# A four-layer modulated convolution on one core: another opening, with filler matmuls on TensorE

## The reference

```
x = out = input                               # (128, 64, 1024)
for i, typ in enumerate(('same', 'upsample', 'same', 'downsample')):
    s = style @ mod_w[i].T + mod_b[i]         # (128, 64)
    weight = SCALE * w[i] * s[:, None, :, None]
    demod  = rsqrt(sum(weight * weight, axis=(2, 3)) + 1e-8)
    weight = weight * demod[:, :, None, None]
    same:       out = conv1d(out, weight, stride 1, pad 1) + b
    upsample:   out = blur(conv_transpose(out, weight, stride 2) + b)
    downsample: out = conv1d(blur(out, pad 2), weight, stride 2) + b
return x + out
```

## Time and profile before

| | us |
|---|---|
| median of 3 runs | 692.41 (690.55 to 693.0) |
| the profiled execution | 691.5 |
| its span | 689.6 |

### The profile page before, as it was taken

The page is one execution under the profiler, slowest core; times in us unless marked ns, Lnnn a source line. Parts: engine busy times, 40 slices in busy tenths (PEclk is TensorE's granted clock), DMA queues, the critical chain, the costliest instruction groups (busy, mean ns, idle before and its releaser), DMA issues.

```text
span 689.6 us, 12124 instructions
## 1 busy us (share of the span) xinstructions
PE 660.8 (96%) x4434; PEld 618.8 (90%) x4434; DVE 471.3 (68%) x705; ACT 313.0 (45%) x499; POOL 374.0 (54%) x392
## 2 busy tenths in 40 slices
PE   5668999999999999999999999999999999999997
PEld 4667899999999999999999999999999999999986
DVE  6867668777675687676757786757666967586551
ACT  3424534544544445454444444444444543545441
POOL 3355555755555646646565555566555565655420
PEclk9989999999999999999999999999999999999999
DMA  7054767876767867756787757678776576877763
GB/s 246 0 116 79 188 179 176 205 179 144 180 170 189 207 146 184 183 157 179 187 207 177 166 145 194 161 194 207 177 175 157 156 190 182 207 177 177 167 156 137
DMA packets 130234, 117.22 MB, mean 170 GB/s; under 512 B 6080, under 2 KB 96576, under 8 KB 130176
## 3 DMA queue, kind: packets, MB, share of 16 engines
q1 hardware_dynamic: 129520, 114.88, 66.7%
q10 hardware_dynamic: 656, 1.57, 0.7%
HBM read 36.47 MB, written 33.82 MB: 102 GB/s over the span
## 4 chain that ended last, share of the span: by engine, by line
PE 95%; DVE 3%; issue 1%; ACT 1%; DMA 1%; POOL 0%; DVEq 0%; POOLq 0%; ACTq 0%
PE po L174 17%; PE po L175 16%; PE po L176 16%; PE pg L174 8%; PE pg L176 8%; PE pg L175 8%; PE pg L179 4%; PE pg L180 4%; PE pm L176 3%; PE pm L174 3%; PE pm L175 3%; PE pe L378 1%; PE pe L371 1%; DMA Gf<-in_st 1%; PE pe L381 0%
## 5 line engine op out<-in xcount | busy, mean ns | idle before, releaser
L174 PE MATMUL po<-xh,W 128*128 128x256 f32 (+1 forms) x640 | 218.2, 341 | 2.4 <-DVE T L682 1.7
L175 PE MATMUL po<-xl,W 128*128 128x256 f32 (+1 forms) x640 | 217.6, 340 | 0.0
L176 PE MATMUL po<-xh,W 128*128 128x256 f32 (+1 forms) x640 | 217.4, 340 | 0.0
L176 PEld LDWEIGHTS po<-xh,W 128*128 128x128 f32 x640 | 126.2, 197 | 12.3
L174 PEld LDWEIGHTS po<-xh,W 128*128 128x128 f32 x640 | 125.6, 196 | 12.3 <-issue 2.7
L175 PEld LDWEIGHTS po<-xl,W 128*128 128x128 f32 x640 | 126.1, 197 | 9.9
L602 POOL TENSOR_TENSOR Q2l<-Q2f,Q2h 128x512 fp32r<-128x512 f32 x31 | 74.0, 2386 | 85.5 <-ACT Q2h L489 85.5
L682 DVE SCALAR_TENSOR_TENSOR T<-po,DD,M 128x512 f32<-128x512 f32 x64 | 48.0, 750 | 82.6 <-PE po L176 51.0
L450 ACT CAST xh<-X 128x1032 fp32r<-128x1032 f32 x64 | 80.9, 1264 | 37.9 <-PE po L176 37.9
L673 DVE TENSOR_TENSOR xl<-X,xh 128x1032 fp32r<-128x1032 f32 x64 | 95.9, 1499 | 2.4 <-ACT xh L450 2.4
L494 ACT CAST Gh<-Gf 128x512 fp32r<-128x512 f32 x64 | 39.8, 621 | 119.0 <-DVE Gf L704 119.0
(11 more groups left out here) (169 smaller groups left out, 1523.2 us busy)
## 6 DMA issues: line engine op xcount, KB each, us to landing
X<-in_xin SPq DMA_DIRECT2D x64, 516.0 KB, 4.4
out<-T SPq DMA_DIRECT2D x64, 512.0 KB, 3.5
W<-W SPq DMA_DIRECT2D x96, 256.0 KB, 4.3
W<-W SPq DMA_DIRECT2D x32, 384.0 KB, 5.6
V<-V SPq DMA_DIRECT2D x32, 128.0 KB, 5.1
V<-W SPq DMA_DIRECT2D x32, 64.0 KB, 3.6
V<-Vx SPq DMA_DIRECT2D x32, 64.0 KB, 2.8
E<-in_ed ACTq DMA_DIRECT2D x1, 768.0 KB, 7.4
```

The costliest lines, as they stand in the source:

```text
L174: eng.matmul(o, wh_, rh, start=first, stop=False)
L175: eng.matmul(o, wh_, rl, start=False, stop=False)
L176: return eng.matmul(o, wl_, rh, start=False, stop=last)
```

## The change

The steady loop stays. The opening is written anew:

- The root comes straight from ScalarE's reciprocal-square-root function, and the Newton step is three operations of VectorE in place of the reciprocal and four. Scales and energies of layers 2 and 3 go first.
- The static sums are done by TensorE: two times nine matmuls against multiples (1, 6, 15, 20) of an identity, into `po[0]` and `po[1]`; VectorE makes three of the multiples. They are rounded from PSUM.
- The inputs arrive in another order and in smaller pieces; ScalarE issues three transfers, not five.
- Group 1's second stage moves into the prologue, group 2's first stage in front of group 1's third; the low parts of group 1's Q2 and G are VectorE's in the opening, not GpSimd's. `x_low(1)` is made one sample earlier, in front of W of group 1.
- Group 0's W crosses in two times four transfers, the columns of samples 0 and 1 first; sample 2 has its own wait.
- 32 matmuls of 512 columns (`warm`), whose results nobody reads, stand in TensorE's order in four blocks of 7, 3, 5 and 17. They read a tile of ones that GpSimd writes at the start.

```diff
-PROLOGUE = [(0, 0), (0, 1), (0, 2), (0, 3), (0, 4), (0, 5), (0, 6), (1, 0), (1, 1)]
-FIRST = [[(1, 2), (1, 3)], [(1, 4), (1, 5), (1, 6)], [(2, 0), (2, 1)], [(2, 2), (2, 3)]]
+PROLOGUE = [(0, u) for u in range(7)] + [(1, u) for u in range(4)]
...
+            def warm(n, at):
+                for _ in range(n):
+                    pe.matmul(at[:, :], WARM[:, 0:128], WARM[:, 128:640], start=True, stop=True)
...
+            pe.wait_ge(s_dm, 1)
+            warm(7, pg[3])
+            pe.wait_ge(s_in["mw2"], 16)
+            pe.wait_ge(s_in["st"], 16)
+            scales(P2)
+            scales(P3).then_inc(s_pp, 1)
+            warm(3, pg[3])
             pe.wait_ge(s_sq, 1)
             pe.wait_ge(s_sc, SC_SQ2)
             energy(2).then_inc(s_pp, 1)
+            pe.wait_ge(s_in["mwt"], 16)
+            scales(0)
+            scales(1).then_inc(s_pp, 1)
+            pe.wait_ge(s_in["b1"], 16)
+            pe.wait_ge(s_ek, 3)
+            static_sums(0).then_inc(s_bp, 1)
             pe.wait_ge(s_sq, 2)
-            pe.wait_ge(s_ss, 1)
+            pe.wait_ge(s_ss, 2)
             for l in (0, 1, 3):
                 m = energy(l)
...
             for x in PROLOGUE[:2]:
                 unit(*x)
+            static_sums(1).then_inc(s_bp, 1)
...
             m.then_inc(s_pp, 1)
+            warm(5, po[1])
             pe.wait_ge(s_cl, 1)
             for x in PROLOGUE[4:9]:
                 unit(*x)
+            warm(17, po[1])
+            for x in PROLOGUE[9:]:
+                unit(*x)
...
             constant(2, 1, SC_K2)
+            conv(0)
+            constant(3, 3, SC_K3)
...
+            def cross_pair(a):
+                w = r32(W[:, 0]).rearrange("p v t a r m -> p (v t) a r m")
+                s = s_wb if a else s_w[0]
+                for part, (i, e, f) in enumerate(((0, 4, 4), (4, 10, 8))):
+                    sp.wait_ge(s_wh, part + 1)
+                    sp.wait_ge(s_wl, part + 1)
+                    sp.dma_start(w[hi, i:e, a, 1], w[lo, i:e, a, 0]).then_inc(s, 16)
+                    sp.dma_start(w[lo, i + 2:f + 2, a, 1], w[hi, i:f, a, 0]).then_inc(s, 16)
...
-            def newton(l):
-                link(tt(tmp[:, l], RR[:, l], RR[:, l], ALU.mult))
-                link(tt(tmp[:, l], tmp[:, l], AA[:, l], ALU.mult))
-                link(dve.tensor_scalar(tmp[:, l], tmp[:, l], -0.5, 1.5, ALU.mult, ALU.add))
-                link(tt(DD[:, l], tmp[:, l], RR[:, l], ALU.mult))
+            def newton(l, t, also=None):
+                link(tt(t, RR[:, l], AA[:, l], ALU.mult))
+                if also:
+                    tt(kt[:], RR[:, l], also[0], ALU.mult)
+                link(dve.scalar_tensor_tensor(out=t, in0=t, scalar=-0.5, in1=RR[:, l], op0=ALU.mult, op1=ALU.mult))
+                if also:
+                    reached(dve.scalar_tensor_tensor(out=also[1], in0=t, scalar=1.5, in1=kt[:], op0=ALU.add, op1=ALU.mult))
+                return dve.scalar_tensor_tensor(out=DD[:, l], in0=t, scalar=1.5, in1=RR[:, l], op0=ALU.add, op1=ALU.mult)
```

More of the change, by code:

```diff
@@ L125, in build @@
         ST = flat3(Gf, 512, 512 + B)
[L126 to L130, removed]
+        EK = [EYE[:]] + [flat3(Wf, 256 * k, 256 * k + 256) for k in range(3)]
+        WARM = xl[:, 1, 0, 0:640]
         Y1 = flat(AA, 0, 13 * EC).rearrange("p (b n) -> p b n", n=13)
@@ L234, in cross_sums @@
                 sp.dma_start(v[lo, 1, :, 1], r32(Vx[hi])).then_inc(s_v[g % 2], 16)
-            for n in range(XR):
-                load(n)
+            load(0)
+            load(1)
+            sp.dma_start(E[:], ed.rearrange("p (l t m) -> p l t m", l=4, t=3)).then_inc(s_in["ed"], 16)
+            load(2)
             sp.dma_start(XE[:], xe).then_inc(s_in["xe"], 16)
-            cross(0, 0)
-            cross(0, 1)
+            cross_pair(0)
+            cross_pair(1)
             cross_sums(0)
@@ L382, in edge, with scales @@
                 m.then_inc(s_e, 1)
[L384 to L388, removed]
+            def warm(n, at):
+                for _ in range(n):
+                    pe.matmul(at[:, :], WARM[:, 0:128], WARM[:, 128:640], start=True, stop=True)
+            def scales(l):
+                return pe.matmul(ps[:, l * 128:l * 128 + 128], MW[:, l, :], ST, start=True, stop=True)
             def energy(l):
@@ L395, in energy, with static_sums, add @@
                 return m
+            def static_sums(d):
+                p = lo if d else slice(0, 128)
+                at = slice(128, 256) if d else slice(0, 128)
+                x = b1t[p]
+                def add(c, i, n, rhs, first, last=False):
+                    return pe.matmul(pb[d][:, i:i + n], EK[c][p, at], rhs, start=first, stop=last)
+                end = x[:, 2:3].to_broadcast([64, 2, C]) if d else x[:, 2:3]
+                end3 = x[:, 3:4].to_broadcast([64, 2, C]) if d else x[:, 3:4]
+                n = 2 if d else 1
+                add(0, 0, 2, x[:, 0:3:2], True)
+                add(2, 2, 2, x[:, 0:3:2], False)
+                add(0, 4, n, end, False)
+                add(0, 3, 1, x[:, 0:1], False)
+                add(2, 1, 2, x[:, 0:3:2], False)
+                add(1, 1, 2, x[:, 1:4:2], False)
+                add(3, 2, 2, x[:, 1:4:2], False)
+                add(1, 3, 1, x[:, 1:2], False)
+                return add(1, 4, n, end3, False, True)
+            pe.wait_ge(s_dm, 1)
[5 more added lines that the diff above has]
+            warm(3, pg[3])
             pe.wait_ge(s_sq, 1)
@@ L540, in _ @@
             high(1, 1)
+            q3_high(2)
+            high(1, 2)
+            high(1, 3)
             sums_high(0)
+            x_high(1)
             for b in range(B):
```

200 lines of the change are left out of this document (99 added, 101 removed).

## The result

| | before | after |
|---|---|---|
| median, us | 691.97 (690.55 to 693.0, 4 runs) | 680.99 (678.67 to 683.02, 4 runs) |
| the profiled execution, us | 691.5 | 678.67 |
| its span, us | 689.6 | 676.8 |

The account below looks back on a forecast made before the run. TensorE is always busy after 73.57 us, so only the opening, bound by waits (mostly for VectorE) and a low clock, can be won. Gain 15.6 less 2.6 for contention is 13.0: 678.5 or 679.4, said as 679.0; range 674.5 to 687.0.

Parts of the forecast that it names:

- off for contention: Opening before 45 us: four VectorE instructions lengthened beside GpSimd take 2.6 us off the gain, 15.6 to 13.0.
- sample 4: First convolution of group 1 (b = 4): starts at 58.0 instead of 73.57, 15.6 us gained before contention.
- Start and root: Opening up to stage 1: first fillers cost 0 to 0.1 us, energy at 6.8, stage 1 at 14.0, 1.9 gained.
- rival B: Clock stays low through the first stages and the fillers block: 4.5 to 7.5 us gained, 684 to 687; chance 0.20.
- Stage 2 and 3 of group 0: Opening: stage 2 starts at 17.9, 4.9 us gained so far; stage 3 at 23.8, 6.0 gained so far.
- Stage 2 of group 1: Opening, Q2's low parts on VectorE: chain 7.7 us instead of 11.4, start 31.5 against 41.15, 9.65 gained so far.
- The fillers: TensorE's opening: first seven cost 0 to 0.1 us; seventeen end 0.1 late at the high clock, 3.4 at the low.
- C: Opening: GpSimd holds VectorE, all 11.6 us of its work standing in the chain: 4.0 us gained, 687.5; chance 0.05.
- D: Cross copies before b = 4 take 11.8 us as before: 8.9 us gained, 682.6; chance 0.09.
- E: Opening's gain is given back at once because group 1 waits for VectorE: 690 to 693 us; chance 0.06.
- F: Steady loop: each later group waits 0.8 us for its cross copies, 31 times, so slower, 703 us; chance 0.04.
- A: The forecast itself, the opening shortened as replayed: 675 to 684 us; chance 0.56.

Follow-up runs that it names:

- the repeat: The kernel after run once more with no edit: 680.0 us (677.63 to 681.54, 5 runs), ratio 0.9817 to the kernel before.
- the improved version: Kernel after with VectorE's edge constants put off until sample 4 and ScalarE evicting sample 2's M before rounding x: 676.56 us, ratio 0.9779 to the kernel before.

## Why the prediction was right, point by point

Forecast 679.0, range 674.5 to 687.0; measured 680.99, and 680.0 in the repeat. The chain and the clock worked as forecast. The last term, 2.6 us off for contention, was right by luck. By step, with the time expected and the time in the first profile:

| step | expected | measured |
|---|---|---|
| layer-2 energy | 6.8 | 6.83 |
| stage 1 | 14.0 | 12.99 |
| stage 2, group 0 | 17.9 | 16.89 |
| stage 3 | 23.8 | 22.73 |
| stage 2, group 1 | 31.5 | 31.40 |
| first convolution | 35.2 | 35.34 |
| sample 2 | 48.5 | 48.96 |
| sample 4 | 60.6 (58.0 + 2.6) | 60.57 |

*Start and root.* Right in kind and 1 us too careful in size. The layer-2 energy starts at 6.83 as forecast, with both blocks low, as I had counted them. In the first profile the clock rose during that energy, at about 7 us (in the others with these fillers between 4 and 7), so its last passes, the second scales and the sums ran high where I had still counted the first two of these low. The "no fillers" run gives the alternative of rival B: 12.2 us before the clock rose. I took the high level because TensorE would have hardly a gap. That reason alone does not carry: without fillers it had no gap either from 5.65 on, and the clock rose at 12 us in two profiles and at 27 in a third. With the first ten fillers it was up by 7.7 us in all eight profiles of the new kernel that have them, so the fillers were the cause.

*Stage 2 and 3 of group 0.* Each gain as priced (4.9 and 6.0, here 5.9 and 7.0, the extra 1 us being that of the start). The reciprocals' removal was counted as chain only. That is true of 2.7 us in the kernel before; in the kernel after the runs showed 5.3, because the wait for VectorE also costs the clock and the fillers then stand in the way.

*Stage 2 of group 1.* The time was right by cancellation. The lead of 1 us at stage 3 was gone here: 8.7 us from there where I had 7.7. VectorE's rows around that stretch are not those of an idle neighbour:

```profile
21.48 1.10 DVE L784 TENSOR_TENSOR Gl<-Gf,Gh 128x512 fp32r<-128x512 f32 x1
...
22.95 0.85 DVE L183 TENSOR_TENSOR Gh<-Gf,Gh 64x256 fp32r<-64x256 f32 x1
...
30.04 1.21 DVE L183 TENSOR_TENSOR Q2h<-Q2f,Q2h 64x256 fp32r<-64x256 f32 x1
31.29 2.02 DVE L732 TENSOR_TENSOR xl<-X,xh 128x1032 fp32r<-128x1032 f32 x1
```

Undisturbed these take 0.68, 0.42, 0.42 and 1.22. Gl ends in front of stage 3, and xl is not waited for by stage 2, so in the stretch itself lie Gh and Q2h, 0.4 and 0.8 us too long. The choice that I held for a gain here, low parts on VectorE, is worth 0.7 at this stage and nothing at sample 4, as its reversal shows.

*Off for contention, and sample 4.* This is where luck came in. The 2.6 us were to stand for four lengthened VectorE instructions on the way. The traces show that the landing of the last cross copy sets sample 4. I had the last issue at 52.7 and 4.3 us to land, so 57.0, and took 58.0. Measured are an issue at 53.43 and 6.9 to land, so 60.33, and a start at 60.57. The difference of 2.57 is 0.7 for the later issue, 2.6 for the landing and 0.2 up to the start, less the 1.0 that I had added. Only the 0.7 can be contention. The landing alone has the size of what I took off for another cause.

The 4.3 is the page's median over all groups. It was the wrong figure for the last of four copies issued in a row: that one took 8.0 us in the kernel before, 6.9 in the kernel after and 7.1 in the improved version, and each time TensorE started 0.2 to 0.3 us behind it.

A second thing was missing from the replay and did no harm. TensorE was ready for sample 4 at 58.84, not 56.7. Of these 2.1 us, 1.28 are the wait for M at sample 3, which no step of mine held, because I followed VectorE and SyncE there and not ScalarE's order, where the cast of x stands in front of M. Without it TensorE would have been ready at 57.56 and would have waited for the crossing until 60.33 all the same.

*The fillers.* Expected: no cost if the clock is high. The 22 later ones cost nothing in the kernel after. The first seven did: the scales start at 4.57 behind them, and at 3.59, 3.46 and 3.45 in the three runs without them, because in the new order the inputs arrive earlier than the 4.33 of before that I used. So this block costs 1.0 to 1.1 us, not 0 to 0.1, and the second some 0.2 more in the first profile; the clock that they raise pays it back (stage 1 at 12.99 against 14.40). What the prediction did not price is what each block is worth. The runs: ten give all that the medians resolve; the other 22 shorten the opening by 1.7 to 1.8 us in both pairs of profiles, and by 0.0 and 1.3 in the medians.

*What separates 678.7 from 681.* The prediction has no step for it. The clock falls in some runs behind the crossing wait and behind the wait for the last T, which cost 1.5 and 1.7 us in the one that was profiled. I worked from one profile against one profile; the median of this program lies above its best run, here by 2.3 and 2.4.

*The rivals.* B did not occur, though the two versions without fillers show that it was near: in the improved one stage 1 starts at 16.22 and stage 2 at 22.79 at the low level. C: partly, in rows of VectorE, not 11.6 us of them; but the sign that I named for being wrong, rows of VectorE twice as long beside GpSimd, did appear (0.85 for 0.42, 1.21 for 0.42). D: the crossing took 9.5 us from its first issue (51.04) to the use, half way between the 6.7 of my replay and the 11.8 of before; its last copy, with 6.9 us, is nearer to the 8.0 of before than to 4.3. I gave this rival 0.09, too little. E and F fell: the loop from 60.57 to 640 has 579.43 of 579.43 us busy.

One slip: the range is said to leave out 0.03 of A, which as written (675 to 684) lies wholly inside it.

Left open: the last wait for the crossing (1.5 us in the best version) was not removed by any run, and whether the later fillers bring 1 us or nothing can't be told at this spread. Of the 7.7 us of the rebuilt chain only the root (2.7 in the kernel before), group 1's low parts and the halved crossing were tried alone. The static sums on TensorE, the order of the inputs, the units moved and the earlier x_low(1) were not; that they make up the rest is argued from the traces.

## What to carry to other kernels

Where an engine's clock depends on what it did before, price an idle gap with what follows it: the reciprocals were worth 2.7 us in a chain that ran low anyway and 5.3 in one that they threw back to the low level (2.4 and 4.6 at sample 4 of the profiles, which say more than two medians with intervals of 1 to 3 us). Cheap dummy work belongs in front of the first real work, sized to the wait there as it will be after the change (seven matmuls were 1 us too many for the new wait, and still paid). Further on it is worth only what no later wait takes back.

When a wait ends with a transfer, take the landing of that very transfer from the trace, not the median of its group: 6.9 to 8.0 us here against 4.3. And a forecast that hits may do so by two errors that cancel: compare it step by step. When a chain gets shorter, walk through every engine's fixed order for the instruction that used to be early enough, here a cast of x in front of M; then ask whether another wait behind it hides what the repair would bring, as the crossing did.

Before one profile is compared with another, find the first point where they part for a reason that is not the edit. Here it was the rise of the clock, worth up to 0.9 us at stage 1.

## What the runs showed of the hardware

VectorE and GpSimd hold each other up by whole instructions in all five pairs below, and did not in the one where VectorE reads from PSUM. GpSimd of the kernel after, in two stretches:

```profile
29.21 1.76 POOL L643 TENSOR_TENSOR X<-X 128x516 f32<-128x516 f32 x1 [4.81 <-issue]
31.05 1.16 POOL L646 TENSOR_TENSOR X<-X 128x516 f32<-128x516 f32 x1
...
42.53 2.43 POOL L666 TENSOR_TENSOR Q2l<-Q2f,Q2h 128x512 fp32r<-128x512 f32 x1 [5.21 <-ACT Q2h L551]
```

VectorE beside the second of them:

```profile
42.05 1.76 DVE L732 TENSOR_TENSOR xl<-X,xh 128x1548 fp32r<-128x1548 f32 x1
43.72 0.28 DVE L860 TENSOR_TENSOR cv<-pe,DD 64x128 f32<-64x128 f32 x1
44.04 1.00 DVE L861 TENSOR_SCALAR cv<-cv,BB 64x128 f32<-64x128 f32 x1
```

GpSimd's first ended at 30.97: VectorE's Q2h, started at 30.04, ended 0.28 us behind it. The second ended at 32.21: xl, started at 31.29, ended 1.10 us behind it. The third ended at 44.96: L861, started at 44.04, ended 0.08 behind. The other way round, xl of 42.05 ended at 43.81, and GpSimd's 512-column product, 1.32 us long when undisturbed (at 55.00), ended 1.15 us after that. But L860, which reads `pe` in PSUM, ran its 0.28 us in the midst of GpSimd's. So whoever starts second does nearly all its work behind the end of the first, less some 0.15 us, and a row's excess can be worked out once both timelines lie side by side. The earlier trace rows read the same way: GpSimd's Cl ran from 10.70 to 11.98 in before, and the product of 0.94 ended at 12.13, 0.15 behind it. The Trainium skill ("SBUF — State Buffer", section "Who interferes with whom") says just this: who issues first has the shared ports for the whole instruction, and an operation of VectorE with at most one input in SBUF does not contend, apart from a mode that some operations enter, TENSOR_SCALAR among them. The five pairs here agree, L861 if it was in that mode, which no row shows. Read rightly before the run, the rule would have priced the lengthened rows of the opening pair by pair.

Nearly the same wait dropped the clock in one execution and left it at 1.00 in another of the same program: 1.90 and 1.73 us at sample 4, 1.8 in both at the last T. A profile at 1.00 shows the best of such a kernel.

The first rise varies as much. With the same 32 or 10 fillers it came between 4 and 7 us. Without them TensorE was busy without a gap from 5.7 or 5.8 us on in three profiles, with the same work, and the clock rose at about 12 us in two and at 27 in the third. The recorded clock shows none of this, since it starts at 1.00; the spacing of matmuls of one shape does.
